# State-space stage of a two-layer model: chunk sums with the operands exchanged and turned back, growth factors by DMA, and the input projection moved into the gates stage

## What is computed

```python
xp = x @ Wx.T
Bm = rope(rmsnorm(x @ WB.T, Bn_w) + B_bias, cumsum(theta * dt))
Cm = rope(rmsnorm(x @ WC.T, Cn_w) + C_bias, cumsum(theta * dt))
dt = softplus(x @ Wdt.T); lam = sigmoid(x @ Wlam.T)
alpha = exp(dt * A); beta = (1 - lam) * dt * alpha; gamma = lam * dt
h = alpha_t * h + beta_t * outer(B_prev, x_prev) + gamma_t * outer(B_t, x_t)
y_t = C_t @ h                       # each head, each token
out = (y * silu(x @ Wz.T)) @ Wout.T
```

## Time and profile before

| | |
|---|---|
| median of three runs | 6169.8 us |
| lowest and highest | 6169.16 and 6174.46 us |
| the profiled execution's own time | 6162.61 us |
| its span, first to last instruction | 6160.8 us |
| busy: PE, PEld, DVE, ACT, POOL | 90%, 64%, 73%, 57%, 59% of the span |
| mean granted clock of PE | 0.945 |
| instructions | 127971 |

### The profile page before, as it was taken

The page is one execution under the profiler, slowest core; times in us unless marked ns, Lnnn a source line. Parts: engine busy times, 40 slices in busy tenths (PEclk is TensorE's granted clock), DMA queues, the critical chain, the costliest instruction groups (busy, mean ns, idle before and its releaser), DMA issues. The chain is left out here.

```text
span 6160.8 us, 127971 instructions
## 1 busy us (share of the span) xinstructions
PE 5549.1 (90%) x40796; PEld 3972.6 (64%) x40796; DVE 4509.5 (73%) x6856; ACT 3505.7 (57%) x4756; POOL 3636.6 (59%) x4101
## 2 busy tenths in 40 slices
PE   5999588459999999999999999999999999984699
PEld 3454277337777777777777777777777777763587
DVE  5777555538888888888888888888888888835444
ACT  2444222227777777777777777777777777731222
POOL 2222000018888888888888888888888888820000
PEclk9889599679999999999999999999999999986799
DMA  3333200131111111111111111111111111121100
GB/s 100 108 114 118 79 18 24 38 121 32 29 29 30 28 34 29 29 29 30 32 28 31 29 32 29 29 31 27 34 29 29 29 30 32 28 90 62 42 24 20
DMA packets 435078, 267.89 MB, mean 43 GB/s; under 512 B 269092, under 2 KB 363876, under 8 KB 434052
## 3 DMA queue, kind: packets, MB, share of 16 engines
q1 hardware_dynamic: 417284, 257.14, 15.1%
q10 hardware_dynamic: 17664, 9.44, 0.5%
HBM read 186.73 MB, written 66.85 MB: 41 GB/s over the span
## 5 line engine op out<-in xcount | busy, mean ns | idle before, releaser
L1564 ACT ACTIVATE ss_r<-ss_pssum,ss_eps 128x512 f32<-128x512 f32 x512 | 352.9, 689 | 901.8 <-PE ss_pssum L1495 901.8
L1624 DVE SCALAR_TENSOR_TENSOR ss_psb<-ss_psb,ss_norm,ss_r 128x512 f32<-128x512 f32 x512 | 362.9, 754 | 446.4 <-ACT ss_r L1566 446.4
L1495 PE MATMUL ss_pssum<-ss_sq,ss_pairssum 128*128 128x512 f32 x1024 | 570.9, 639 | 57.7 <-DVE ss_fr L1612 57.7
L1376 POOL TENSOR_TENSOR ss_sq<-ss_sq 128x512 f32<-128x512 f32 x256 | 329.6, 1287 | 451.6 <-ACT ss_sq L1573 451.6
L48 PE MATMUL ss_psb<-x_hi,ss_whi 128*128 x1024 | 529.5, 517 | 4.4 <-DVE ss_fr L1612 4.4
L1476 PE MATMUL ss_psse<-ss_rot 64*128 64x128 f32 x8224 | 530.0, 279 | 0.3 <-POOL ss_rot L1358 0.3
L1406 POOL TENSOR_TENSOR ss_own<-ident,ss_tk 128x512 f32<-128x512 f32 x512 | 524.4, 1045 | 0.0
L1476 PEld LDWEIGHTS ss_psse<-ss_rot 64*128 64x128 f32 x8224 | 480.6, 188 | 43.6 <-issue 43.0
L48 PE MATMUL ss_psc<-x_hi,ss_whi 128*128 x1024 | 506.6, 495 | 0.0
L1366 POOL TENSOR_TENSOR ss_sq<-ss_sq 128x512 f32<-128x512 f32 x256 | 325.1, 1270 | 136.0 <-ACT ss_sq L1580 136.0
L50 PE MATMUL ss_psb<-x_hi,ss_wlo 128*128 x1024 | 403.7, 394 | 0.0
(11 more groups left out here) (346 smaller groups left out, 15582.3 us busy)
## 6 DMA issues: line engine op xcount, KB each, us to landing
ss_dtb<-time_steps SPq DMA_DIRECT2D x516, 128.0 KB, 2.9
ss_wraw<-in_w_state SPq DMA_DIRECT2D x264, 80.0 KB, 2.3
head_rows<-a_yhi SPq DMA_DIRECT2D x64, 256.0 KB, 2.5
a_qs<-head_rows SPq DMA_DIRECT2D x128, 96.0 KB, 2.2
a_ks<-head_rows SPq DMA_DIRECT2D x128, 96.0 KB, 2.2
ss_xp<-x_heads SPq DMA_DIRECT2D x33, 256.0 KB, 4.2
y_heads<-ss_yo SPq DMA_DIRECT2D x132, 64.0 KB, 2.4
head_rows<-a_ylo SPq DMA_DIRECT2D x32, 256.0 KB, 2.7
```

The costliest lines, as they stand in the source:

```text
L1376: G.tensor_tensor(sq[:, 0, 0], sq[:, 0, 0], sq[:, 0, 1], ALU.add).then_inc(ss_b, 1)
L1495: M(p_sum[:], pairs_sum[:], sq[:, q, 0], start=True, stop=True).then_inc((sum_b, sum_c)[q], 1)
L1564: A(r[:, q], p_sum[:], ACT.Ln, scale=1.0 / N1, bias=eps[:, 0:1]).then_inc(ln, 1)
L1624: link.mark(S(bank[:, e, :], bank[:, e, :], norm[:, 2 * q + e:2 * q + e + 1], r[:, q], ALU.mult, ALU.mult))
```

## The change

In the gates stage the input projection is added and its own stage is dropped: SP loads its weights once the gate weights are split, DVE splits them, PE runs the 32 tiles right behind the gate projections, without staging x, into four banks, and ACT copies them out in groups between its functions; two buffers and one store for each tile stay. In the state space three things are exchanged. The growth factors no longer go through PE and ACT: SP loads them already spread, four DMAs a turn, two turns ahead of use. The chunk sums take x as the loaded operand (32 columns, three column groups) and B as the streamed one, so that the result lies turned; DVE masks it into SBUF, PE turns it back (turn_sums, behind squares(k, 1)), and only then DVE copies the first entering state, behind masked(k). The rest of the turn's order is as it was.

```diff
 (state_space, SP)
 def load_rows(pair, i, j):
-    sp.dma_start(grown[:, j, :], grown_dram[ds(j * H1 + pair * 2, 2), ds(i * SEQ, SEQ)]).then_inc(rows_in[j], 16)
...
+def load_growth(pair, i, j):
+    for c in range(TPB):
+        source = grown_dram[ds(j * H1 + pair * 2, 2), ds(i * SEQ + c * P, P)].rearrange("h (o t) -> h o t", o=1)
+        sp.dma_start(grown[32 * c:32 * c + PW, j, :], source.broadcast_to([2, P1, P])).then_inc(growth_in[j], 16)
...
     load_rows(pair, i, j)
+    latest = (u + UNITS - 1) % UNITS
+    sp.wait_ge(y_ready, u)
+    load_growth(latest // BATCH, (latest // 2) % (BATCH // 2), 1 - j)
     sp.wait_ge(thdt_done, u + 1)
 (POOL: same products, written to the middle of a wider tile)
-G.tensor_tensor(xe[:, j].rearrange("p c (h d) -> p (c h) d", d=P1), xp_u,
-                tk_of(1).broadcast_to([P, 8, P1]), ALU.mult).then_inc(xk_done, 1)
+G.tensor_tensor(xe[:, j, :, PW:2 * PW].rearrange("p c (h d) -> p c h d", d=P1),
...
 (PE, turn_b)
-if e == 0:
-    for c in range(TPB):
-        last = M(bank[32 * c:32 * c + 32, 3 * P:4 * P], heads[:], grown[:, 1 - j, c * P:(c + 1) * P],
-                 start=True, stop=True)
 (PE, chunk_sums)
-for c in range(3):
-    for e in range(2):
-        last = M(p_m[:, (c * 2 + e) * PW:(c * 2 + e + 1) * PW], bt[:, 2 if e else j, c, :], xe[:, 1 - j, c, :],
-                 start=True, stop=True)
+for e in range(2):
+    for c in range(3):
+        last = M(p_m[32 * c:32 * c + 32, 3 * P:4 * P], xe[:, 1 - j, c, (1 - e) * PW:(3 - e) * PW],
+                 bt[:, 2 if e else j, c, :], start=e == 0, stop=e == 1)
+def turn_sums(k):
+    pe.wait_ge(um_done, k + 1)
+    T(p_m[:, 0:6 * PW], sums[:], g.ident[0:96, 0:96]).then_inc(ut_done, 1)
...
     squares(k, 1)
+    turn_sums(k)
 (ACT, take_b)
-n = TPB - e
-A(bt[:, 2 if e else j, 0:n, :], bank[:, 0:n * P]..., ACT.Copy).then_inc(taken[e], 1)
+A(bt[:, 2 if e else j], bank[:, 0:3 * P]..., ACT.Copy).then_inc(taken[e], 1)
 (DVE, combine)
+dve.wait_ge(growth_in[j], loads)
-link(V.tensor_tensor(inter[:], p_m[:, P:2 * P], bt[:, 1 - j, TPB - 1, :], ALU.mult))
+link(V.tensor_tensor(inter[:], p_m[:, P:2 * P], grown[:, j], ALU.mult))
 (DVE, states)
 dve.wait_ge(u_done, k + 1)
-sums = p_m[:, 0:6 * PW].rearrange("p (g d) -> p g d", d=PW)
-link(V.tensor_tensor(sums, sums, blocks[:].rearrange("p (o d) -> p o d", o=1).broadcast_to([P, 6, PW]), ALU.mult))
+V.tensor_tensor(sums[:], p_m[0:96, 3 * P:4 * P], block_rows[:], ALU.mult).then_inc(um_done, 1)
-link.mark(V.tensor_copy(entering(1), added[:, 0]))
-moved = link.n
 masked(k)
-link.wait(moved)
+dve.wait_ge(ut_done, k + 1)
+link(V.tensor_copy(entering(1), added[:, 0]))
 link(S(entering(2), entering(1), ends[:, ds(at + 1, 1)], added[:, 1], ALU.mult, ALU.add))
 S(entering(3), entering(2), ends[:, ds(at + 2, 1)], added[:, 2], ALU.mult, ALU.add).then_inc(s_ready, 1)
```

```diff
 (gates_and_heads; input_projection and its stage are dropped)
 (SP)
+sp.wait_ge(w_split, 2)
+sp.dma_start(x_raw, wx_d).then_inc(loaded, 16)
+for t in range(TILES):
+    sp.wait_ge(x_taken, t + 1)
+    sp.dma_start(xp_v[t], heads[:, t % 2]).then_inc(x_out[t % 2], 16)
 sp.wait_ge(rows_ready, 1)
 (PE, behind the gate projections; px is four banks)
+for t in range(TILES):
+    if t >= 4:
+        pe.wait_ge(x_taken, t - 3)
...
+        last = matmul3(nc, px[t % 4][:], g.x_hi[:, k, tok], g.x_lo[:, k, tok], x_whi[:, k], x_wlo[:, k],
+                       k == 0, k == KD - 1)
 (ACT)
+def take_heads(t):
+    act.wait_ge(x_done, t + 1)
+    if t >= 2:
+        act.wait_ge(x_out[t % 2], 16 * (t // 2))
+    A(heads[:, t % 2], px[t % 4][:], ACT.Copy).then_inc(x_taken, 1)
 A(lam[:], lam[:], ACT.Sigmoid).then_inc(act_sem, 1)
 A(dt[:], z[:], ACT.Abs).then_inc(act_sem, 1)
+take_heads(0)
 A(ea[:], ea[:], ACT.Exp).then_inc(act_sem, 1)
 A(dt[:], dt[:], ACT.Exp, scale=-1.0).then_inc(act_sem, 1)
+take_heads(1)
 A(dt[:], dt[:], ACT.Ln, bias=1.0).then_inc(act_sem, 1)
+for t in range(2, TILES // 2):
+    take_heads(t)
 act.wait_ge(dve_to_act, 1)
 A(tmp[:], tmp[:], ACT.Exp).then_inc(act_sem, 1)
+for t in range(TILES // 2, TILES):
+    take_heads(t)
 act.wait_ge(dve_to_act, 2)
 A(lam[:], cum[:], ACT.Exp).then_inc(quantity, 1)
```

More of the change, by code:

```diff
@@ L868, with gates_and_heads @@
 WCH = WC // BATCH
-def gates(nc, ctx, w_d, alog_d, tk_dram, dt_dram, grown_dram, decay_dram, ends_dram, g):
+def gates_and_heads(nc, ctx, w_d, alog_d, wx_d, xp_dram, tk_dram, dt_dram, grown_dram, decay_dram, ends_dram, g):
     sem = lambda n: nc.alloc_semaphore(name=f"ga_{n}")
@@ L891, in gates @@
         pt = [ps(f"t{i}", [P, 4, P]) for i in range(2)]
+        px = [ps(f"x{i}", [P, DIN]) for i in range(4)]
+        xp_v = xp_dram.rearrange("(n p) d -> n p d", p=P)
         block = mem.enter_context(nc.Block())
@@ L910, in _ @@
             sp.wait_ge(stored, 112)
+            for p in range(2):
+                sp.wait_ge(x_out[p], 16 * (TILES // 2))
         @block.tensor
@@ L924, in _ @@
                 last.then_inc(z_done, 1)
+            pe.wait_ge(x_split, 2)
+            for t in range(TILES):
+                if t >= 4:
+                    pe.wait_ge(x_taken, t - 3)
+                tok = slice(t * P, (t + 1) * P)
+                for k in range(KD):
+                    last = matmul3(nc, px[t % 4][:], g.x_hi[:, k, tok], g.x_lo[:, k, tok], x_whi[:, k], x_wlo[:, k],
+                                   k == 0, k == KD - 1)
+                last.then_inc(x_done, 1)
             for n in range(12):
@@ L1001, in _ @@
             V.tensor_copy(part[:, 2, :], keep[:]).then_inc(rows_ready, 1)
[L1003 to L1065, removed]
@@ L1187, in state_space @@
     rows_in, dt_in, wraw_in, pair_in, y_out = ([sem(f"{n}{p}") for p in range(2)] for n in ("rows", "dt", "wraw", "pair", "yout"))
-    th_done, b_done, c_done, sum_b, sum_c, e_done, s_done, u_done, yp_done = (
-        sem(n) for n in ("th", "b", "c", "sumb", "sumc", "e", "s", "u", "yp"))
+    growth_in = [sem(f"growth{p}") for p in range(2)]
+    th_done, b_done, c_done, sum_b, sum_c, e_done, s_done, u_done, ut_done, yp_done = (
+        sem(n) for n in ("th", "b", "c", "sumb", "sumc", "e", "s", "u", "ut", "yp"))
     turned = [sem("turn0"), sem("turn1")]
@@ L1193, in state_space @@
     taken = [sem("taken0"), sem("taken1")]
-    y_ready, thdt_done, fr_done, rope_b, rope_c, s_ready, gm_done, chain_sem = (
-        sem(n) for n in ("yready", "thdt", "fr", "ropeb", "ropec", "sready", "gm", "chain"))
+    y_ready, thdt_done, fr_done, rope_b, rope_c, um_done, s_ready, gm_done, chain_sem = (
+        sem(n) for n in ("yready", "thdt", "fr", "ropeb", "ropec", "um", "sready", "gm", "chain"))
     ss_b, ss_c, rot_b, rot_c, dd_done, xk_done, own_done, pool_chain = (
@@ L1659, in _ @@
                     phases(k + 2, 1 - j, (n + 1 + j) * 32, link)
-                    combine(k, j, (older // BATCH) % 2, older % BATCH, link)
+                    combine(k, j, (older // BATCH) % 2, older % BATCH, (n + j) * 64, link)
                     rotate(k, j, k // BATCH, 0, link)
@@ L2035, in state_constants @@
     blocks = (t[:, None] // H1 == np.arange(PW)[None, :] // P1).astype(np.float32)
-    heads = (np.arange(2)[:, None] == np.arange(32)[None, :] // P1).astype(np.float32)
-    return left, right, strict, np.ascontiguousarray(blocks), heads
+    return left, right, strict, np.ascontiguousarray(blocks), np.tile(blocks.T, (6, 1))
 @contextmanager
@@ L2062, in program @@
         with phase(nc):
-            gates(nc, ctx, i["w_dt"], i["a_log"], tk, dt, grown, decay, ends, g)
-        with phase(nc):
-            input_projection(nc, ctx, i["w_x"], xp, g)
+            gates_and_heads(nc, ctx, i["w_dt"], i["a_log"], i["w_x"], xp, tk, dt, grown, decay, ends, g)
         with phase(nc):
             state_space(nc, ctx, i["w_state"], i["state_norm"], i["state_bias"], i["left"], i["right"], i["strict"],
-                        i["blocks"], i["heads"], tk, dt, grown, decay, ends, xp, y, g)
+                        i["blocks"], i["block_rows"], tk, dt, grown, decay, ends, xp, y, g)
         with phase(nc):
```

40 lines of the change are left out of this document (27 added, 13 removed).

## The result

The changed kernel takes 6330.07 us (median of four runs, 6327.04 to 6331.6), the kernel before beside it 6172.13 us. The ratio is 1.0256 with a 95% interval of 1.024 to 1.0273: slower, as forecast, one microsecond from the predicted 6329. The profiled execution took 6331.14 us against 6162.61 us, so 168.5 us more. Two executions of later runs lie far above all others and no ratio uses them: 10595.5 us of the first kernel of part 8 and 7781.5 us of the kernel before, beside part 5.

What follows compares the result with a forecast made beforehand. The loop over DVE was taken as the bound, PE having 0.23 us a turn to spare: 6162.6 - 52 (gates) + 212 (copy and offset arithmetic) = 6322.6, with the medians' 7 us 6329 us; range 6255 to 6410 us.

Steps and rivals of the forecast that it cites:

- The bound: State-space stage: the loop over DVE sets the pace, and PE has 0.23 us a turn to spare.
- The step that costs: DVE in the state space: late copy 0.23 us plus bared offset arithmetic 0.60, 0.83 us a turn, +212 us.
- The price of a step: Offset arithmetic on DVE: 0.048 us a step, from L1617's 0.48 us for ten; 0.62 and 0.58 us here.
- Gates: Gates stage: dropping the projection's own stage saves 58.4 us, ACT's copies cost 6; together -52 us, -56 to -48.
- PE's wait: State space: PE's wait for fr_done grows from 57.7 us to some 500 us in total.
- the term of PE's savings: PE in the state space: about 1.3 us less work a turn, outside fr_done to L1646, counted at 0 us.
- The cover of the mask: DVE's mask writes 128 columns instead of 96 ahead of L1646: 0 us, up to 0.1 us of cover left.
- The clock: State space: PE's longer pauses lower its clock in one turn of three, +136 us, 6465 us; chance 0.15.
- (a): State space: PE is the bound or DVE has slack, so the copy costs nothing; 5778 to 6111 us; chance 0.04.
- (b): DVE in the state space: offset arithmetic is done ahead of the wait, +59 us, 6177 us; chance 0.05.
- (c): State space: PE's turned sums come after L1646's end, at most 0.1 us a turn, 6355 us; inside the main case.

Runs made afterwards that it cites:

- part 8: Kernel before with only the growth factors exchanged: 6171.7 us; changed kernel with six more unread PE transposes a turn: 6330.83 us.
- part 5: Changed kernel with nine more register steps, result unused, behind the wait for the copy of the first entering state: 6336.79 us.
- run 4: Changed kernel with the offset arithmetic of both ends done earlier, between combine and the rotation of B, copy left in place: 6194.37 us.
- runs 6 and 7: Seven more register steps in the decays' offset, in the changed kernel: 6413.89 us; the same in the kernel before: 6172.84 us.

## Why the prediction held, and where it didn't

- **The bound.** Held. The 57.7 us of waits of a PE that was busy for 98% of its stage named the bound rightly, and both runs of part 8 show it: outside the stretch from fr_done to the masked scores PE may do 0.35 us less or 0.65 us more in a turn.
- **The step that costs.** Held. Predicted 0.83 us a turn and +212 us; measured +213.2 in the stage (0.83 a turn), +212.2 by the medians, and +220 for that edit alone. The first state starts 0.87 and 0.78 us behind the copy's start in the two halves, 0.825 on average, against the 0.83 of copy and arithmetic together. Working the offsets out ahead gives back 0.53 of it (run 4), and 0.30 stay.
- **The price of a step.** Right in sum, and by luck. The prediction read the offset of L1617 in one half of the loop only, at 0.80 us behind L1616 in the earlier trace rows. In the other half, which is also the turn of the earlier trace rows, the same ten steps of program text cost less:

```profile
3424.31 0.28 DVE L1616 TENSOR_TENSOR ss_inter<-ss_psm,ss_bt 128x128 f32<-128x128 f32 x1
3424.84 0.29 DVE L1617 TENSOR_TENSOR ss_yo<-ss_psm,ss_inter 128x128 f32 x1 [0.24 <-DVE ss_inter L1616]
...
L1617 DVEq FUSED_REGOPS  x384: 135/157/293, 1377.3 to 5422.1; - x192
```

That is 0.53 us, so 0.21 for ten steps instead of 0.48: one fused register operation in this half, two in the other. By the mean of both halves a step is 0.035 us, 12.5 steps are 0.43, and the same sum gives 0.66 us a turn, +169 us and 6287. The slower half happened to fit: L1640's offset has two such operations, and somewhat longer ones, in both halves. A count of steps in the program's text is no measure of them; the rows of DVE's sequencer on L1640, which the trace of before already had, are.
- **Gates.** Predicted -52, measured -53.5 alone and -55.0 in the stage, from two errors that partly cancel. ACT's stretch ahead of the exponential of cum was 44.4 us, where the prediction had 45 less about 3 for the buffers that are free, so 42; the exponential came 6.8 us later in its stage, where it had some 6. Then 3.5 us came back behind it, which the prediction had at nothing.
- **PE's wait.** This was wrong in size: "some 500 us in total" for fr_done, measured 278.3. The step that failed is the term of PE's savings: the chunk sums measured 0.64 us and not 0.47, turning back 0.25 and not 0.16, so 1.04 us a turn by the rows and not 1.3, and 0.82 by PE's busy time. And I put all of PE's idle time at one wait. The stage has 4270 - 3802 = 468 us of it, but 74.6 stand before the squares of C, which now wait for POOL, 34.1 before a half of C that waits for the rotation, and 80.5 before a half of B in every second turn, for which the profile names no releaser; what holds it was not settled. It cost the sum nothing, as PE's time was priced at 0.
- **The cover of the mask.** I gave it 0.1 us; it has 0.42, because the copy, which used to stand there, had left.
- **The clock.** The rival at 0.15 did not come. PE now pauses for 0.96 us (1.33 in the other half) before L1483 and 0.29 before the squares of C, turn after turn, and the granted clock of the stage stays 1.00. The Trainium skill, "TensorE: Matmul & The Clock Gate", section "A second HAM failure mode: psum-queue depth-cycling", tells of another kernel in which small idles of PE between groups of matmuls made the clock swing. This trace shows no such swing for these pauses.
- **The other rivals.** (a), PE as the bound, fell by part 8. (b), the arithmetic ahead of the wait, is not what this program does, but run 4 makes it so and lands at 6194, 17 us above the 6177 that I gave. (c), turned sums late, is true only once the copy stands ahead of the masked scores (0.40 and 0.64 us of waiting in the rows above); behind them it costs nothing.
- The nearness of 6329 to 6330 is luck in good part: the price of a step came from the half of the loop that happened to fit, worth 43 us, and the errors of the gates stage cancel to 1.5 to 3 us. That the kernel would be some 3% slower, and by which wait, is not: it follows from the place of the copy and of the arithmetic.

## What to carry to other kernels

Here an engine that was busy for 98% of its stage was not the bound: it waited 0.23 us in every turn for the same neighbour, and work saved on it outside the stretch that the neighbour waits for turned into a longer wait. Before an instruction is moved on the engine that does set the pace, ask what ran underneath its old neighbours: here the arithmetic of a computed address was hidden under a 1.2 us instruction, and moving a 0.19 us copy by one place laid it bare, 0.65 us of idle in each of 256 turns. Work out such offsets where the engine waits anyway, and read what they cost from the register operations of the engine's sequencer on that line, not from the program's text.

## What the runs showed that I had not expected

- Seven more register steps in an offset cost 0.33 us a turn where nothing covers them, and nothing under a long instruction (runs 6 and 7). Steps that nobody reads vanish in compilation (run 5).
- A chained wait with a single register step behind it still takes 0.36 us from start to start for an instruction of 0.24, against 0.39 with three; with fixed addresses it is 0.30 for one of 0.27 (L1634 in the earlier trace rows).
- Four DMAs that spread two rows over partitions take SP 3.26 us a turn to issue, 0.81 each, and hold up nobody:

```profile
3034.66 3.26 SPq L1261 DMA_DIRECT2D ss_grown<-growths  x4
```

- Twelve column-tiled float32 matmuls of 128 columns took 0.64 us, where the sixteen in 0.62 of the earlier trace rows would give 0.47. The twelve lie on three column groups and the sixteen on four, so both are four instructions to a group, and L1464's eight on four groups, two to each, took 0.42. A time that goes by the instructions of one group would fit all three; no run tries it.
